# Quadrant-shaped attention matmuls and a W1 product in 64-column halves, in a conv/attention + mixture-of-experts block on one core

## What is computed

```python
x_tri = windows_of(dct_w(dct_h(layer_norm(x))))          # [image, window, 64 positions, 16]
q, k, v = l2norm(x_tri @ Wq), l2norm(x_tri @ Wk), x_tri @ Wv   # norm over the 64 positions
attn = softmax((q^T k) * rescale)                        # 16 x 16 for each window and head
x_low = (attn v) @ proj_w + proj_b
h1 = gelu(depthwise3x3(gelu(conv1x1(x_dct)))); x_conv = h1 + x_dct
x_high = gelu(conv1x1(x_conv)) + x_conv
x = x + idct(coef * x_low + (1 - coef) * x_high + x_dct)
# 8 experts, top 2, on tokens of 64 features
h = gelu(xe @ W1[e] + b1[e]); y = h @ W2[e] + b2[e]      # 64 -> 256 -> 64
out = sum over the two picked experts of weight * y
```

## Time and profile before

| | us |
|---|---|
| median of 3 runs | 260.94 |
| lowest, highest | 260.77, 261.13 |
| the profiled execution | 260.44 |
| its span in the trace | 258.4 |

### The profile page before, as it was taken

The page is one execution under the profiler, slowest core; times in us unless marked ns, Lnnn a source line. Parts: engine busy times, 40 slices in busy tenths (PEclk is TensorE's granted clock), DMA queues, the critical chain, the costliest instruction groups (busy, mean ns, idle before and its releaser), DMA issues.

```text
span 258.4 us, 3162 instructions
## 1 busy us (share of the span) xinstructions
PE 228.3 (88%) x1206; PEld 117.9 (46%) x1206; DVE 151.1 (58%) x266; ACT 129.8 (50%) x206; POOL 47.0 (18%) x44
## 2 busy tenths in 40 slices
PE   2857699999996967978479999999999999999993
PEld 2744589848462655977333223223223332333230
DVE  0791849999797798777993424424424433443344
ACT  1246741003508064166447566567567666766670
POOL 3850095003562048003300000000000000000000
PEclk9995999999997999999759999999999999999999
DMA  6970000000000000000009315080511707062001
GB/s 232 256 196 0 3 0 4 0 0 0 3 0 1 0 0 3 0 0 3 0 22 232 85 44 128 0 203 3 134 28 42 164 0 164 0 143 63 0 0 41
DMA packets 6590, 14.18 MB, mean 55 GB/s; under 512 B 2736, under 2 KB 4144, under 8 KB 5680
## 3 DMA queue, kind: packets, MB, share of 16 engines
q1 hardware_dynamic: 6576, 13.99, 22.0%
HBM read 12.81 MB, written 1.18 MB: 54 GB/s over the span
## 4 chain that ended last, share of the span: by engine, by line
PE 79%; DVE 12%; ACT 6%; DMA 1%; issue 1%; SPq 0%; DVEq 0%
PE psum L623 24%; PE psum L638 23%; PE psum L482 6%; PE psum L454 3%; PE psum L464 3%; PE psum L422 2%; DVE place L985 2%; ACT place L673 2%; PE psum L570 2%; ACT place L667 2%; PE psum L552 2%; PE psum L395 1%; PE psum L536 1%; PE psum L445 1%; PE psum L490 1%; PE psum L561 1%
## 5 line engine op out<-in xcount | busy, mean ns | idle before, releaser
L780 ACT ACTIVATE hid<-psum,b1p 128x512 f32<-128x512 f32 x128 | 77.8, 688 | 40.5 <-PE psum L623 40.5
L1075 DVE SCALAR_TENSOR_TENSOR term<-psum,sm,wide 128x512 f32<-128x512 f32 x32 | 24.0, 751 | 71.8 <-PE psum L638 71.8
L623 PE MATMUL psum<-tok,w1s 128*128 128x512 f16 x256 | 64.8, 390 | 0.0
L638 PE MATMUL psum<-hid,w 128*64 128x512 f32 x256 | 61.8, 604 | 0.0
L623 PEld LDWEIGHTS psum<-tok,w1s 128*128 128x128 f16 x256 | 22.0, 100 | 51.4 <-ACT hid L780 27.4
L638 PEld LDWEIGHTS psum<-hid,w 128*64 128x64 f32 x256 | 15.6, 136 | 32.0 <-issue 27.0
L1080 DVE TENSOR_TENSOR x<-x,term 128x512 f32<-128x512 f32 x32 | 22.2, 692 | 1.1
L482 PE MATMUL psum<-h_pad,tap_bd 128*128 128x512 f32 x36 | 15.8, 592 | 0.0
L395 PE MATMUL psum<-c,xs 128*128 128x128 f32 x32 | 7.6, 431 | 5.6 <-DMA xs<-in_x 5.6
L907 DVE SCALAR_TENSOR_TENSOR place<-h_pad,sm,place 128x512 f32<-128x512 f32 x16 | 12.0, 752 | 0.6
L482 PEld LDWEIGHTS psum<-h_pad,tap_bd 128*128 128x128 f32 x36 | 6.7, 189 | 8.2 <-issue 8.2
(11 more groups left out here) (135 smaller groups left out, 293.4 us busy)
## 6 DMA issues: line engine op xcount, KB each, us to landing
wide<-gate_store SPq DMA_DIRECT2D x14, 512.0 KB, 6.3
xs<-in_x SPq DMA_DIRECT2D x2, 512.0 KB, 5.1
w1f<-in_W SPq DMA_DIRECT2D x2, 512.0 KB, 9.6
block_out<-x SPq DMA_DIRECT2D x4, 256.0 KB, 6.5
wide<-gate_store SPq DMA_DIRECT2D x2, 384.0 KB, 5.0
hid<-in_W1T SPq DMA_DIRECT2D x1, 512.0 KB, 10.4
w<-in_W SPq DMA_DIRECT2D x1, 512.0 KB, 12.0
c<-const SPq DMA_DIRECT2D x1, 483.5 KB, 4.2
```

The lines of the kernel that those rows point to most:

```text
L623: mm = pe.matmul(h_bank(n), w1s[:, part, e, k * P:(k + 1) * P], tok[:, pair, half, b, :], start=part == 0, stop=part == 1)
L638: mm = pe.matmul(y_bank(u)[b * H:(b + 1) * H, :], w2[:, e * KT + k, :], hid[:, u % 2, B2 * k + b, :], start=k == 0, stop=k == KT - 1)
L780: act.activation(hid[:, u % 2, t, :], h_bank(n), ACT.Gelu, bias=b1p[:, e * KT + k:e * KT + k + 1]).then_inc(gelu_ready, 1)
L1075: dve.scalar_tensor_tensor(term[:, u % 2, :], y_bank(u), b2t[:, e:e + 1], gate_b[part][:, e % (E // 2), :], ALU.add, ALU.mult).then_inc(te ...
```

## The change

- `gram_matrices`: each product of 64 rows x 128 columns becomes two of 64 x 64, only the two diagonal halves of the 128 x 128 result are made, and the Gram matrices are kept as 64-wide blocks. DVE masks 512 columns at a time instead of 1024, and starts when all 32 products of a pair are done rather than half of them.
- `gram_times_w`, `norms`, `logits`, `project`, `low`: products over 128 rows with block-diagonal weights become two products over 64 rows each (rows 0 to 63 and 64 to 127). In the first four, half of the windows have the halves of their partitions crossed on the way (`crossed`), so that all four quadrants of the array are used. `times_wv` uses quadrants too and `mask_mix` handles 512 columns at a time.
- `norms` writes its result in two PSUM banks instead of one. `second_taps` uses the second of these banks, so it now waits for a new semaphore `norms_read`, which DVE gives in `inverse_norms` when it has read the norms.
- In the table, `logits` goes to turns (16, 21) and `second_taps` to (17, 22): they trade places.
- `up`: each 128-column product becomes two of 64 columns, to the two halves of the partitions.
- `softmax_in` multiplies by the norms of k in two halves of 512 columns; a constant `half_mask` of 64 columns is added.

```diff
-    "second_taps": (16, 21), "logits": (17, 22),
+    "second_taps": (17, 22), "logits": (16, 21),
...
             def gram_matrices(p):
                 pe.wait_ge(halo_ready, p + 1)
-                for j in range(2):
-                    pe.wait_ge(xt_ready, 2 * p + j + 1)
-                    for q in range(4):
-                        for odd in range(2):
-                            v = xt[p][odd * H:(odd + 1) * H, (4 * j + q) * P:(4 * j + q + 1) * P]
-                            mm = pe.matmul(slot(p, j)[:, (4 * odd + q) * P:(4 * odd + q + 1) * P], v, v, start=True, stop=True)
-                    mm.then_inc(gram_done, 1)
+                pe.wait_ge(xt_ready, 2 * (p + 1))
+                for q in range(K):
+                    for half in range(2):
+                        for odd in range(2):
+                            v = xt[p][rows_of(odd), q * P + half * H:q * P + (half + 1) * H]
+                            mm = pe.matmul(bank(slot(p, 1), odd)[rows_of(half), q * H:(q + 1) * H], v, v, start=True, stop=True)
+                mm.then_inc(gram_done, 1)
...
             def norms(p):
...
                 for d in range(DH):
-                    mm = pe.matmul(slot(p, 0)[:, 0:2 * G * HEADS], const("pick")[:, DH - 1 - d:DH - 1 - d + P], columns[:, d, :, :],
-                                   start=d == 0, stop=d == DH - 1)
+                    for swapped in range(2):
+                        for half in range(2):
+                            first = DH - 1 - d + half * H
+                            mm = pe.matmul(bank(slot(p, 0), swapped)[rows_of(crossed(half, swapped)), 0:side],
+                                           const("pick")[rows_of(half), first:first + H],
+                                           columns[rows_of(half), d, swapped], start=d == 0, stop=d == DH - 1)
...
             def second_taps(p):
-                pe.wait_ge(tk_ready, 2 * p + 1)
+                pe.wait_ge(norms_read, p + 1)
...
             def low(p):
...
-                    mm = pe.matmul(slot(p, 0)[:, g * H:(g + 1) * H], mix[p][:, parity(g), :], xd[p][:, g * H:(g + 1) * H], start=True, stop=True)
+                    for half in range(2):
+                        mm = pe.matmul(slot(p, 1)[rows_of(half), g * H:(g + 1) * H], mix[p][rows_of(half), mix_index(g), :],
+                                       xd[p][rows_of(half), g * H:(g + 1) * H], start=True, stop=True)
...
             def up(u):
...
                     for part in range(2):
-                        mm = pe.matmul(h_bank(n), w1s[:, part, e, k * P:(k + 1) * P], tok[:, pair, half, b, :],
-                                       start=part == 0, stop=part == 1)
+                        for side in range(2):
+                            mm = pe.matmul(h_bank(n)[side * H:(side + 1) * H, :],
+                                           w1s[:, part, e, k * P + side * H:k * P + (side + 1) * H], tok[:, pair, half, b, :],
+                                           start=part == 0, stop=part == 1)
...
             def inverse_norms(p):
...
-                link(dve.tensor_scalar(r[:, 3, :], slot(p, 0)[:, 0:2 * G * HEADS], NORM_EPS ** 2, None, ALU.max))
+                dve.tensor_scalar(split(r[:, 3, :], G * HEADS), split(slot(p, 0), CHUNK)[:, :, 0:G * HEADS],
+                                  NORM_EPS ** 2, None, ALU.max).then_inc(norms_read, 1)
+                dve.wait_ge(norms_read, p + 1)
```

More of the change, by code:

```diff
@@ L47 @@
     "gram_matrices": (11, 12), "gram_times_w": (13, 14), "first_taps": (3, 7), "norms": (15, 19), "mask_gram": (4, 5),
-    "second_taps": (16, 21), "logits": (17, 22), "products": (6, 8), "keep_tk": (11, 13), "inverse_norms": (9, 14),
+    "second_taps": (17, 22), "logits": (16, 21), "products": (6, 8), "keep_tk": (11, 13), "inverse_norms": (9, 14),
     "scale_logits": (11, 15), "norms_of_k": (18, 26), "softmax_in": (12, 17), "gelu_second": (12, 20),
@@ L112, in constants @@
     out[:, CONST["shifted"]] = block
+    out[:, CONST["half_mask"]] = np.tile(np.kron(np.eye(H // C), np.ones((C, C))), (2, 1))
     out[:, CONST["diagonal"]] = np.tile(np.eye(DH), (P // DH, 1))
@@ L176, in split, with crossed, rows_of, mix_index @@
             return v.rearrange("p (g h) -> p g h", h=n)
-        def parity(g):
-            return g // K * K + g % 2 * 4 + g % K // 2
+        def crossed(half, swapped):
+            return 1 - half if swapped else half
+        def rows_of(half):
+            return slice(half * H, (half + 1) * H)
+        def mix_index(g):
+            depth, column, odd = g // K, g % K // 2, g % 2
+            return column % 2 * K + depth * 4 + 2 * odd + column // 2
         c32 = sb("c32", [P, CONST_N])
@@ L242, in metaformer @@
         attn = tk
-        gram = [wide[0][:, p, :].rearrange("p (g n) -> p g n", n=P) for p in range(PAIRS)]
+        gram = [wide[0][:, p, 0:N].rearrange("p (g n) -> p g n", n=H) for p in range(PAIRS)]
         spread_k = [wide[0][:, p, 0:N] for p in range(PAIRS)]
@@ L247, in metaformer @@
         prod = [wide[1][:, p, :].rearrange("p (g n) -> p g n", n=P) for p in range(PAIRS)]
-        mix = [wide[1][:, p, :].rearrange("p (g n) -> p g n", n=P) for p in range(PAIRS)]
+        mix = [wide[1][:, p, 0:N].rearrange("p (g n) -> p g n", n=H) for p in range(PAIRS)]
         h_early = [bank(slot(0, 1), 0), bank(slot(0, 1), 1), bank(slot(0, 0), 1)]
@@ L471, in logits @@
                 pe.wait_ge(bd_ready, 1)
+                tk_of = tk[p].rearrange("p (h s n) -> p s h n", h=HEADS, s=2)
+                n = K * DH
                 for h in range(HEADS):
-                    mm = pe.matmul(slot(p, 1)[:, h * G * DH:(h + 1) * G * DH], wq_bd[:, h, :],
-                                   tk[p][:, h * G * DH:(h + 1) * G * DH], start=True, stop=True)
+                    for swapped in range(2):
+                        for half in range(2):
+                            mm = pe.matmul(bank(slot(p, 1), swapped)[rows_of(crossed(half, swapped)), h * n:(h + 1) * n],
+                                           wq_bd[rows_of(half), h, rows_of(half)], tk_of[rows_of(half), swapped, h],
+                                           start=True, stop=True)
                 mm.then_inc(logit_done, 1)
             def second_taps(p):
-                pe.wait_ge(tk_ready, 2 * p + 1)
+                pe.wait_ge(norms_read, p + 1)
                 pe.wait_ge(bd_ready, 1)
@@ L502, in project @@
             def project(p):
[L504 to L508, removed]
-                    if h % 2:
-                        mm.then_inc(y_done, 1)
+                n = K * DH
+                for swapped in range(2):
+                    pe.wait_ge(attn_ready, 2 * p + swapped + 1)
+                    for h in range(HEADS):
+                        for half in range(2):
+                            mm = pe.matmul(bank(slot(p, 0), swapped)[rows_of(crossed(half, swapped)), h * n:(h + 1) * n],
+                                           proj_bd[rows_of(half), h, rows_of(half)],
+                                           bank(attn[p], swapped)[rows_of(half), h * n:(h + 1) * n], start=True, stop=True)
+                    mm.then_inc(y_done, 1)
             def heads(p):
```

76 lines of the change are left out of this document (44 added, 32 removed).

## The result

The changed kernel takes 263.26 us (median of 4 runs, 262.80 to 263.92) beside 260.97 us: a ratio of 1.009, 95% interval 1.0067 to 1.0114. It is slower by 2.3 us, by more than the 0.2% that a measurement tells; the forecast was 262.0 with 257 to 266 around it. Its profiled execution took 263.1, with a span of 261.1.

A forecast was written before the change was run, and what follows sets the result against it. PE was taken to set the experts' pace and most of the middle, DVE the part from 84.65 to 100.53 us. +8.8 in front and -7.8 behind made +1.0, 262.0 us against the median; eight in ten 257.0 to 266.0.

The forecast's parts named there:

- The experts: `up` and `down`: equal shapes save 0.25 us a unit in 31 of 32 units, -7.8 us.
- the clock at their head: First expert units: more low clock than the 4.0 us met before, +0.5 us.
- The open question: `up` and `down`: whether the 0.25 us a unit comes from the shape change or from fp16 to float32.
- The first wait: `second_taps(0)` behind DVE's read of the norms: PE stands still 5 to 6 us, taps start at 51.4, +1.1.
- The second wait: `second_taps(1)` behind DVE's read at 77.9: PE stands still 8 us, taps start at 78.25 and end +14.4.
- The clock behind the waits: Second taps of both pairs: half speed after each standstill loses 2.95 us for each new wait.
- What is given back: Logits already done, shorter projection, `times_wv(0)`, `norms_of_k(1)` and `low(1)` bring +14.4 down to +7.4 us.
- one more stretch of low clock somewhere: Between 92 and 112 us, where PE has half the work between the same waits: +0.9 us (0 to 1.7).
- the bound of 25 ns: `norms(1)`: records start no faster than the router's, 25 ns apart, so 128 records take 3.2 us; 2.5 was taken.
- The cheap clock: Rival at the two waits: each costs 1.2 us of clock instead of 2.95, no further stretch, 257.1 us; chance 0.26.
- The slow experts: Rival in the experts: the type change costs most of the 0.25, only 0.1 a unit won, 266.7 us; chance 0.11.
- the halves that do not share: Rival in `up`: its halves do not share the array, 1.73 us more a unit, +55, 317 us; chance 0.03.

The follow-up runs named there:

- the kernel without the wait: Changed kernel with norms of crossed windows in the first bank of slot (p, 1), taps ahead of logits, logits waiting for the read: 248.90 us, ratio 0.955.
- the filler experiment: Changed kernel plus 5 and 11 float32 matmuls, results unread, in the two standstills ahead of the second taps: 258.74 us, ratio 0.991.
- the one with the biases moved: Norms in the other slot, plus the summing of the experts' biases on DVE moved ahead of the first mask (turn 3, not 10): 252.06 us, ratio 0.970.

## Why the prediction was right, and where it was off

**The experts: right to a tenth.** Forecast 3.45 and 3.60 a unit, measured 3.45 and 3.62; forecast -7.8 and +0.5 for the clock at their head, measured -7.4 together. That the sum fits is in part luck: low clock reached 2.9 us into the experts (to 145.1, first `up` at 142.25), less than the 3.8 of before, so the 0.5 did not come, and a unit gave 0.24 to 0.25. The open question, whether 0.25 us a unit belonged to the change of shape or of data type, is settled: `up` in fp16 and `down` in float32 still take turns, and nothing is left over. The fast weight load that the Trainium skill says is given up ("TensorEngine Tiling (Array Packing)", Restrictions) is not missed in the time: 16 records of `up` take 1.73 us, as 8 did within their stream.

**The first wait: right in kind.** Taps of pair 0 at 52.42, forecast 51.4. DVE read the norms at 52.08 instead of 51.05, because everything up to `gram_matrices` came 1.65 us later than before (`places` of pair 1 at 36.43 instead of 34.78); a shorter mask (2.49 us, forecast 2.75) gave part of it back. The late start is one more stretch of low clock, in a part that the change doesn't touch:

```profile
32.50:35.90 3.40, 3.40 (x7) 1.60 (x6) 3.37 (x2) 1.41 (x3) 3.27 (x1) 0.50 0.00 0
```

The standstill itself was 4.26 and not 5 to 6, since PE stood still for 1.54 us in the middle of `norms` already (below).

**The second wait: right.** `conv_out(0)` forecast 67.3, measured 67.10. Taps of pair 1 forecast 78.25, measured 78.08; projection of pair 0 forecast at about 88.95, measured 88.86 in the chain. The clock behind the waits: forecast 2.95 for each, measured 2.25 and 3.05 (9.98 and 10.78 less 7.73). At the first the taps ran at low clock for 4.0 us, to 56.4, at the second for 5.6, to 83.7. That `conv_out(0)` came to the tenth is luck: the late start of 1.0 was made up for by 0.7 less of low clock and by `norms(1)` at 2.02 instead of 2.5. The mechanism is shown by more than its place: the wait put into the kernel before costs 14.7, taken out of the changed kernel it gives back 14.4.

**What is given back: the term that was too small.** I had `times_wv(0)` at 0.9 and `norms_of_k(1)` at 1.75 us, and 0.9 for one more stretch of low clock somewhere. They met one: 1.62 and 3.08, where the kernel without the wait takes 1.15 and 1.93 at full clock, so this stretch alone cost 1.6. ACT's gap ahead of them, which I had left as it was, grew by 0.5 (88.86 + 1.04 to 93.48, before 78.02 to 81.07). So the softmax of pair 1 began at 98.27 and not at 95.8. Another stretch fell on `project(1)` at 104.2 and cost nothing: from the softmax to `to_frequencies(0)` the chain lies on DVE and takes 13.98, before 13.80. `to_frequencies(0)` started at 112.25, 11.7 later than before where I had 9.2. The gain of `low(1)` came (2.01 for 3.79). Up to the experts I forecast +8.3 and 10.1 came. These missing 1.8 are the whole difference between the forecast of +1.0 and the +2.7 of the profiled executions (the experts gave 0.1 back); between the medians it is 2.3, and 1.3 are missing.

The mechanism and most of its terms held; the closeness of the total owes something to chance. Of the +10.1, 1.65 lie ahead of `gram_matrices`, where nothing was changed and no term of mine stood. From there on +8.5 came for a forecast of +8.3, because what I overrated (the mask, the clock behind the first wait, `norms(1)`) stood against what I underrated.

**The speed of small matmuls.** I took 2.5 us for `norms` between 1.9 and 3.2. 128 records took 2.02 [chain], 16 ns each, so the bound of 25 ns from the router's row (26 by that row itself) does not hold for records across quadrants. The 60 cycles for each matmul, which I cited from the Trainium skill (page "TensorEngine Tiling (Array Packing)", Performance Considerations), I had put on every record. But a float32 product is two records: the 64 products of `norms` start 32 ns apart, above 25 ns, so this trace doesn't show that figure to be wrong for a product, only that my 3.2 us was too much. That made no difference to the loss, as norms and logits were followed by a standstill.

**The rivals.** The cheap clock (257.1) did not come: the two waits lost 5.3 us of clock together and not 2.4. What it would have been worth shows in the filler experiment, which gives 258.7. The forecast's bound, under 260.4 while the waits cost under 2.4 together, is tighter than its own sum asks: by that 4.3 is enough (the 5.9 taken, less 262.0 - 260.4 = 1.6). 5.3 is above either. The slow experts and the halves that do not share are refuted by every profile.

## What to carry to other kernels

When a matmul stage is moved to another PSUM bank, ask who writes that bank next on TensorE and behind whom that engine then stands: here a read of 0.3 us on DVE, queued behind a softmax, held up 8 us of independent convolution and a projection behind it. TensorE can pay twice for such a standstill: behind those of 4.26 and 7.99 us the clock stayed low for the first 4.0 and 5.6 us of the work that followed, behind one of 3.33 us it did not fall, and with the fillers it fell behind 2.58. And in a loop that alternates two shapes of weights on the array, give both the same shape: 0.25 us a turn was there for an edit of three lines.

## What the runs showed of the hardware

A pair of changes of the array's shape between dense streams, 128 to 64 columns and back, costs 0.25 us (a unit of 3.70 against 3.45), about 0.10 of it in `up` and 0.15 in `down`. A change from fp16 to float32 at equal shape costs nothing that shows (1.73 and 1.72 us, the times of the streams alone).

Four quadrants of 64 x 64 take one float32 record of 64 columns every 16 ns (`gram_matrices`: 128 records in 2.10 us), and one of 128 columns every 29 to 31 ns (`gram_times_w`: 128 in 3.72 to 3.95).

In six of the nine versions with `norms` in quadrants PE stops in the middle of `norms(0)`, after 106 of the 128 records each time, for 1.0 to 1.8 us; `norms(1)` runs through. The timeline of the changed kernel:

```profile
43.35 1.81 PE L484 MATMUL psum<-wide,c 64*64 64x64 f32 x106
46.71 0.51 PE L484 MATMUL psum<-wide,c 64*64 64x64 f32 x19 [1.54 <-issue]
```

It waits for nothing that the profile shows. The changed kernel has 15 packets of instruction loading where the kernel before has 9, so the loading of instructions may be it; I did not test that. Against it, the version with the fillers and the one with the biases moved have 15 packets too and no such stop. In the changed kernel the time is hidden in the standstill that follows, and without the wait the chain lies on DVE there.
